# Two of four probability tiles turned by VectorE and transfers instead of TensorE, in 21 plain steps of a fused attention and expert kernel, with a new order of the plain steps

## The reference, cut to what matters

```python
q = (hidden_states @ Wq).reshape(B, Sq, H, D)          # H = 16 heads of D = 128
k = (encoder_hidden_states @ Wk).reshape(B, Skv, H, D)
v = (encoder_hidden_states @ Wv).reshape(B, Skv, H, D)
q = rmsnorm(q, gq)
k = rmsnorm(k, gk)
scores = jnp.einsum('bqhd,bkhd->bhqk', q, k) * scale
attn = jax.nn.softmax(scores, axis=-1)
out = jnp.einsum('bhqk,bkhd->bqhd', attn, v)
return out.reshape(B, Sq, H * D) @ Wo
```

## Time and profile before

| | |
|---|---|
| median of 3 runs | 1463.31 us |
| span of the profiled execution, first to last instruction | 1461.5 us |
| TensorE busy (matmul) | 1437.8 us, 98% |
| VectorE, ScalarE, GpSimd busy | 76%, 67%, 59% |
| granted TensorE clock, mean | 0.998 |

### The profile page before, as it was taken

The page is one execution under the profiler, slowest core; times in us unless marked ns, Lnnn a source line. Parts: engine busy times, 40 slices in busy tenths (PEclk is TensorE's granted clock), DMA queues, the critical chain, the costliest instruction groups (busy, mean ns, idle before and its releaser), DMA issues.

```text
span 1461.5 us, 23763 instructions
## 1 busy us (share of the span) xinstructions
PE 1437.8 (98%) x8086; PEld 1223.0 (84%) x8086; DVE 1107.0 (76%) x2100; ACT 977.5 (67%) x2224; POOL 864.5 (59%) x701
## 2 busy tenths in 40 slices
PE   8999999999999999999999999999999999999998
PEld 6778788888888888888888888888888888888887
DVE  7888777777777777777777777777777776787777
ACT  7864477777776667667676767667676765666664
POOL 4785555555554566666575757575666655664341
PEclk9999999999999999999999999999999999999999
DMA  8420011111111333434333433433434331321002
GB/s 325 159 66 16 22 44 45 57 44 44 44 44 44 139 124 126 149 108 147 124 129 127 139 123 127 139 117 132 136 115 144 125 126 36 107 82 37 8 1 87
DMA packets 55495, 142.74 MB, mean 98 GB/s; under 512 B 5392, under 2 KB 5392, under 8 KB 55376
## 3 DMA queue, kind: packets, MB, share of 16 engines
q1 hardware_dynamic: 51616, 128.90, 26.1%
q0 software_dynamic: 3760, 12.32, 3.0%
HBM read 126.79 MB, written 14.42 MB: 97 GB/s over the span
## 4 chain that ended last, share of the span: by engine, by line
PE 82%; DVE 7%; ACT 4%; POOL 4%; issue 2%; DMA 0%; ACTq 0%; SPq 0%; DVEq 0%; POOLq 0%
PE w_bank L505 10%; PE w_bank L507 10%; PE w_bank L506 10%; PE j_bank L505 9%; PE j_bank L507 9%; PE j_bank L506 9%; PE t_bank L573 7%; PE s_bank L505 4%; PE s_bank L507 4%; PE s_bank L506 4%; PE t_bank L538 2%; POOL q_scale L1855 2%; POOL wo_lo L1815 2%; ACT prob L927 1%; PE t_bank L657 1%
## 5 line engine op out<-in xcount | busy, mean ns | idle before, releaser
L927 ACT ACTIVATE prob<-s_bank,neg_bias,q_scale 128x512 f32<-128x512 f32 x255 | 198.0, 777 | 186.5 <-DVE neg_bias L1422 186.4
L1262 DVE TENSOR_TENSOR probT_lo<-t_bank,probT_hi 128x512 fp32r<-128x512 f32 x260 | 176.4, 689 | 168.4 <-ACT probT_hi L892 168.4
L1476 DVE SCALAR_TENSOR_TENSOR x_sb<-w_bank,inv_sum,x_sb 128x512 f32<-128x512 f32 x254 | 188.4, 744 | 0.0
L1401 DVE TENSOR_REDUCE neg_max<-s_bank 128x1 f32<-128x512 f32 x255 | 168.6, 682 | 0.9 <-PE s_bank L507 0.9
L1815 POOL TENSOR_TENSOR xnT_lo<-xnT_raw,xnT_hi 128x512 fp32r<-128x512 f32 (+2 forms) x47 | 126.5, 2693 | 61.5 <-ACT xnT_hi L892 61.5
L573 PE MATMUL t_bank<-ident,prob 128*128 128x128 f32 x1008 | 151.4, 273 | 1.3 <-ACT prob L927 1.1
L892 ACT CAST probT_hi<-t_bank 128x512 fp32r<-128x512 f32 x260 | 150.1, 590 | 1.8 <-PE t_bank L515 1.8
L1855 POOL TENSOR_TENSOR q_scale<-q_ss,minus_half 128x4 f32<-128x4 f32 x64 | 65.9, 1030 | 143.6 <-DVE q_ss L1414 143.6
L505 PE MATMUL j_bank<-wkv_lo,cT_hi 128*128 128x256 f32 x512 | 145.1, 283 | 0.7 <-DVE oT_lo L1262 0.4
L507 PE MATMUL j_bank<-wkv_hi,cT_lo 128*128 128x256 f32 x512 | 144.6, 282 | 0.0
L506 PE MATMUL j_bank<-wkv_hi,cT_hi 128*128 128x256 f32 x512 | 144.4, 282 | 0.0
(11 more groups left out here) (308 smaller groups left out, 4454.2 us busy)
## 6 DMA issues: line engine op xcount, KB each, us to landing
stage<-w SPq DMA_DIRECT2D x96, 256.0 KB, 3.4
xnT_raw<-w_gu SPq DMA_DIRECT2D x31, 704.0 KB, 4.8
cT_raw<-w_gu SPq DMA_DIRECT2D x31, 704.0 KB, 4.7
xnT_raw<-w_dn SPq DMA_DIRECT2D x16, 768.0 KB, 4.4
cT_raw<-w_dn SPq DMA_DIRECT2D x15, 768.0 KB, 4.7
planes<-bits SPq DMA_DIRECT2D x16, 512.0 KB, 4.8
y<-stage SPq DMA_DIRECT2D x31, 256.0 KB, 4.0
x_sb<-x SPq DMA_DIRECT2D x5, 1024.0 KB, 10.9
```

The costliest lines, as they stand in the source:

```text
L927: nc.scalar.activation(prob[:, i, :], score_bank(t, i)[:], ACT.Exp, bias=neg_bias[:, u % 2, i:i + 1], scale=q_scale[:, u % 2, i:i + 1], ac ...
L1262: return nc.vector.tensor_tensor(dst, src, hi, ALU.subtract)
L1401: nc.vector.tensor_reduce(neg_max[:, u % 2, i:i + 1], score_bank(t, i)[:], AX_X, ALU.max, negate=True).then_inc(own_max, 1)
L1476: nc.vector.scalar_tensor_tensor(out=here, in0=w_bank[0][:] if packed else out_bank(t, i)[:], scalar=inv_sum[:, w % 2, i:i + 1], in1=here, ...
```

## The change: two tiles by another way, a new order of the plain steps, and weights split a step ahead

1. In steps 3 to 18 and 58 to 62 (21 steps, `moved(u)` with u = t-1) tiles 0 and 1 of the probabilities are not turned by TensorE. Their exponentials are written with keys and groups in another order; VectorE turns 32 by 32 blocks in place (`turn_quads`, one instruction of 128 x 1024); SP stores the two tiles to a DRAM scratch (`store_pair`, 512 KB) and loads them back in four transfers of 32 partitions each, in rows of 512 B (`load_pair`); in the next step ScalarE copies them (`moved_hi`, 128 x 1024) and GpSimd subtracts (`moved_lo`, 128 x 1024).
2. `probT` now holds, in all steps, each tile as runs of 32 query columns; `values` reads 16 runs of 32 columns at a distance of 512 B as its moving operand.
3. All plain steps stand in a new order on TensorE, ScalarE, VectorE and SP. `values` writes `t_bank[1]` in them, where it wrote `j_bank[0]`.
4. The key and value weights of item t+1 are split in step t, where they were split at the head of step t+1, in the plain and in the packed steps.

```diff
+def moved(u):
+    return 3 <= u + 1 < T0 - 1 or T0 + NB + 7 <= u + 1 < NI - 1
+def turned_tiles(u):
+    return (2, 3) if moved(u) else range(NT)
...
+        probT_keys = [t[:, :, :].rearrange("p i s -> p (i s)").rearrange("p (q j c) -> p j q c", j=NT, c=QUAD)
+                      for t in probT]
...
+            def store_pair(u):
+                if not moved(u):
+                    return
+                sp.wait_ge(p_quads, MOVES[u] + 1)
+                wait(sp, p_moved, 16 * NT * MOVES[u])
+                sp.dma_start(turn_dram.rearrange("i p m -> p i m"), prob_pair).then_inc(p_stored, 16)
+            def load_pair(u):
+                if not moved(u):
+                    return
+                sp.wait_ge(p_stored, 16 * (MOVES[u] + 1))
+                for c in range(NT):
+                    sp.dma_start(prob[c * QUAD:(c + 1) * QUAD, 0:2, :].rearrange("a i (r m) -> a (i r) m", r=NT),
+                                 turn_dram.rearrange("i (r a) (c m) -> c a (i r) m", r=NT, c=NT)[c]).then_inc(p_moved, 16)
...
+                store_pair(t - 1)
+                load_pair(t - 1)
...
                 def values():
-                    need(pe, p_lo, 4, w, 4)
+                    wait(pe, p_lo, TILES[w + 1])
+                    wait(pe, pair_lo, MOVES[w + 1])
...
-                        last = product(j_bank[0][:], [a[:, w % 2, 1, j * P:(j + 1) * P] for a in kv],
-                                       [a[:, j, :] for a in probT], j == 0, j == NT - 1)
+                        last = product(whole_values(t)[:].rearrange("p (q c) -> p q c", c=QUAD),
+                                       [a[:, w % 2, 1, j * P:(j + 1) * P] for a in kv],
+                                       [a[:, j] for a in probT_keys], j == 0, j == NT - 1)
...
+                def moved_hi(v):
+                    if not moved(v):
+                        return
+                    act.wait_ge(p_moved, 16 * NT * (MOVES[v] + 1))
+                    need(act, pv_mm, 1, v - 1, 1)
+                    copy_hi(probT_pair(0), prob_pair).then_inc(pair_hi, 1)
...
+                def turn_quads():
+                    if not moved(u):
+                        return
+                    need(dve, p_exp, 4, u, 2)
+                    flat_pair = prob_pair.rearrange("p i s -> p (i s)")
+                    nc.vector.transpose(flat_pair, flat_pair).then_inc(p_quads, 1)
...
+                def moved_lo(v):
+                    if not moved(v):
+                        return
+                    pool.wait_ge(pair_hi, MOVES[v] + 1)
+                    lower(probT_pair(1), prob_pair, f32(probT_pair(0))).then_inc(pair_lo, 1)
```

More of the change, by code:

```diff
@@ L782, in step @@
                 scores(1)
-                if not (up and down):
+                if not packed:
+                    project_down()
+                    key_value(0, (0,))
+                    query_squares()
+                    key_value(0, (1,))
+                    late_turn()
+                    key_value(1)
+                    values()
+                    if t == 2:
+                        table()
+                    scores(2)
+                    scores(3)
+                    query((0, 1))
+                    project_out(0)
+                    probs(0)
+                    project_out(1)
+                    probs(1)
+                    probs(2)
+                    query((2, 3))
+                    key_turn()
+                    project_out(2)
+                    probs(3)
+                    project_out(3)
+                    return
+                if not down:
                     query_squares()
@@ new lines, in step @@
+                if t == T0 - 1:
+                    dve.wait_ge(x0_out, 16)
+                    dve.wait_ge(rstd_ready, NMOMENTS // NT + 1)
+                    for i in range(NT):
+                        normalised(i)
+                turn_quads()
+                if t == 2:
+                    tokens()
+                values_lo()
+                take(0)
+                if t == T0 - 2:
+                    statistics(0, 1, NMOMENTS + 1)
+                maximum(2)
+                shift(2)
@@ new lines, in step @@
+                maximum(3)
+                shift(3)
+                add(0)
+                add(1)
+                values_rows()
+                if t == T0 - 2:
+                    statistics(0, 2, NMOMENTS + 2)
+                    statistics(0, 3, NMOMENTS + 3)
+                    for i in range(NT):
+                        mean_variance(0, i, NMOMENTS + i)
+                if t == T0 - 1:
+                    nc.vector.memset(h_row[:, I:], 0.0).then_inc(pad_ready, 1)
+                take(1)
@@ L1715, in _ @@
+                probs_lo(0)
+                probs_lo(1)
+                probs_lo(2)
+                query_lo()
+                key_lo()
+                if t == NI - 1:
+                    last_squares_lo()
+                take(2)
+                add(2)
+                take(3)
+                probs_lo(3)
+                if not deferred(t):
+                    add(3)
             for kind, b in DVE_ORDER:
@@ L1934, in step @@
                 values_lo()
+                if t + 1 < NI and fresh(t + 1):
+                    lower_wkv(t + 1)
                 if t == T0 - 1:
```

290 lines of the change are left out of this document (139 added, 151 removed).

## The result

The changed kernel takes 1471.24 us, the median of 13 runs (1467.96 to 1478.23), where the kernel before took 1464.8 in 13 runs on the same chip: a ratio of 1.0054, 95% interval 1.004 to 1.0068. The forecast was 1436 us, in a range of 1427 to 1450. The change makes the kernel slower by 6 us, and the prediction was wrong in size and in sign.

A forecast was written before the change was run, and what follows sets the result against it. TensorE was taken to bound the kernel. Gains of 21.0 (steps 3 to 18), 4.2 (58 to 62) and 2.1 (52 to 57) made 27.3: 1461.5 - 27.3 = 1434.2, plus 1.8 for the median, 1436 us; range 1427 to 1450.

The forecast's parts named there:

- The step that failed: Plain steps that move no tile: steps 52 to 57 gain 2.1 us, steps 2, 19, 51 and 63 left unchanged.
- 0.25 left over: Delay on TensorE in a late plain step: of 0.6 us, 0.25 was kept as remaining under the new order.
- What it removes on TensorE: Two turned tiles less at 0.44 us each: 0.88 us in each of 21 steps, 18.5 us in all.
- the period of moved steps: Length of a step that moves tiles: 16.3 us for a late one, 16.0 for the others.
- The round trip: Pair's loop through DRAM and back, step to step: 15.6 to 16.6 us against a 16.35 us TensorE step; just in time.
- the long case: Pair's loop when the store waits behind the weights' bytes: 1 us more, 16.6 us.
- the first rival: Moved steps: the pair's loop through DRAM sets the period, fresh steps take 17.2 us, kernel 1455; chance 0.18.
- The four loads: Loads of 128 KB issued some 0.4 us apart, the last landing like a small one: 4.0 us.
- The rival's own terms: Loads landing one behind the other: 10.8 us in place of 4.0, loop 22.4 in 21 steps, about 1560; chance 0.02.
- The values' operand: Runs of 32 columns read by 756 `values` matmuls: taken to cost 0, at most 0.12 us each, 91 us.
- the slower rival: Runs of 32 slow the 756 `values` matmuls: up to 1527 us, deciding from 0.036 us a matmul; chance 0.07.
- Weights a step ahead: Packed steps, earlier split of key and value weights: costed at nothing, up to 0.5 us in each of 10 steps otherwise.

The follow-up runs named there:

- Experiments 1: Changed kernel with steps 19, 51 to 57 and 63 back in the order of the kernel before, `values` in its old bank there: 1459.2 us, ratio 0.9973.
- 4: Changed kernel with no tile going by transfers: new order in all plain steps, four tiles turned on TensorE in each; 1520.8 us, measured once.
- experiment 6: Changed kernel with tile 2 turned behind the second half of the queries in plain steps that turn four tiles on TensorE: 1461.8 us, measured once.
- the fastest kernel: Changed kernel with old order in steps 51 to 57, runs of 32 only for moved items, pair ahead of weights, tile 2 later in 2, 19, 63: 1443.16 us.
- experiment 7: Changed kernel with the store and loads of the pair issued on SP ahead of the query and output weights: 1466.97 us, ratio 1.0015.
- 2: Changed kernel with the runs of 32 columns only in the 21 moved items, other items in one run of 512: 1469.16 us, ratio 1.0035.

## Why the prediction was wrong, step by step

- **The step that failed:** "Steps 52 to 57 [...] the work is 17.0 - 0.44 = 16.55, with 0.25 left over 16.8: 2.1. The remaining plain steps (2, 19, 51, 63) I leave." It put the new order in those steps down as a small gain or nothing. Measured: +16.8 for steps 50 to 57 where -2.1 was forecast, and +1.9, +0.8 and +1.7 for step 19, step 63 and steps 1 and 2 where 0 was: 23.3 of the 35.2 us between the forecast sum and the profiled result. (The others are the start, 3.2, steps 3 to 18, 5.5, and the packed steps, 3.1, with 0.1 in the rest.) I placed the new list for a moved step only, two tiles in it, and carried its "0.25 left over" to steps with four. It could have been seen ahead: the order of the changed kernel shows two adds and a copy of the value rows ahead of tile 0's subtraction on VectorE, and tile 2 on the same bank. Experiments 1, 4 and 6 show it: with the old order back the loss is gone, with no tile moved it stands in every step, and with tile 2 alone shifted more than half of the wait goes and a third of the loss. So the order is shown as the cause of nearly the whole (14.8 of 16.8 us), and the wait of tile 2 by itself as the cause of that third; for the rest it is the longest wait on the list, 13.5 of 16.7 us.
- **What it removes on TensorE, and the period of moved steps:** right. With the store ahead of the weights late steps take 16.27 (16.3), steps 16 and 17 15.82 (16.0), the first and the last of the sixteen 16.7 and 16.9, and all sixteen 260.5, against 259.6 in the sum.
- **The round trip:** its parts were right and its verdict half right. "Just in time, with nothing to spare in the long case" was the finding, and then the long case was costed at nothing. The store behind the weights took 4.0 in the median (forecast 4.5, quiet 3.5; measured quiet 2.8), and the steps where it came late cost 4.5 us in steps 3 to 18. So the first rival came true in a few steps, beside the forecast.
- **The four loads:** last landing 1.81 - 0.45 + 2.7 = 4.1 after the first issue, forecast 4.0. The rule of the Trainium skill, page "DMA: Bandwidth & Descriptors", section "Rules for kernel authors", that ranges of partitions share the engines, may hold for their bytes; as a rule on time the trace doesn't bear it out, since four loads issued within 1.8 us each took 2.7, and the 9 us estimated from the page did not come. The page's 2 us for the fixed part are a fit to transfers that GpSimd issues, and these are SP's. (The rival's own terms, a step of 22.4 in 21 steps, come to 1567, not to "about 1560".)
- **The values' operand:** taken at 0, measured at 0.009 to 0.011 us a matmul, about 4 us in all. The mechanism of the slower rival exists, at a quarter of its deciding point of 0.036. The Trainium skill, page "SBUF — State Buffer", section "Specifications (TRN2)", has it cost nothing by the rule of two hits a 16-byte line; the measurement differs by 4% of a matmul's pace, and decides.
- **Weights a step ahead:** no cost seen. With the runs of 32 taken away the packed steps take 23.50, against 23.48 before; the first packed step is 0.6 shorter.
- **The rival for slower** named the wrong mechanism: a slower operand, not an order that two kinds of step share. Of the chance of 0.09 for slower, 0.07 rested on it and 0.02 on loads that land one behind the other; none rested on the order.

What stays open: in the fastest kernel steps 1 and 2 are 1.0 us longer than before and steps 50 to 57 1.7, of which the mark is 0.7 each; the rest wasn't followed up. Nor were the 9 us by which the stretch of experiment 6 stays behind the old order. How often the clock falls behind a wait, and in which runs, is open too.

## What to carry to other kernels

When one list of instructions serves two kinds of step, walk the new order through each kind, above all the one the change isn't made for: ask of every shared buffer who reads it last and what stands ahead of that reader in its engine's list. A sum that says "just in time" is a term and not a zero; first put the urgent transfer ahead of those that have a whole step. Busy time falling while the span grows says at once that it is a wait; the list of waits of one stretch names it in a line.

## What the runs showed of the hardware

- **A wait can be followed by a fall of the clock.** In the run of experiment 7, the wait of tile 2 in step 55 was followed by matmuls at the lower level, 1.2 GHz, and so was the one in step 56 (TensorE, both waits):

```profile
1299.34 0.63 PE L639 MATMUL t_bank<-ident,prob 128*128 128x128 f32 x4 [2.09 <-DVE probT_lo L1370]
...
1320.73 0.98 PE L639 MATMUL t_bank<-ident,prob 128*128 128x128 f32 x4 [2.45 <-DVE probT_lo L1370]
```

The stretches behind the first (the third figure from the end is the granted clock, 1.00 being 2.4 GHz):

```profile
1299.80:1301.50 1.70, 1.70 (x8) 1.33 (x7) 0.69 (x1) 0.59 (x1) 0.00 (x0) 0.67 0.00 0
1301.50:1303.20 1.70, 1.70 (x8) 1.41 (x7) 0.47 (x1) 0.82 (x2) 0.00 (x0) 0.50 0.00 0
1304.90:1306.60 1.70, 1.70 (x10) 1.41 (x9) 1.70 (x3) 0.23 (x1) 1.55 (x2) 1.00 0.03 10
```

The two steps took 1.5 and 1.1 us more than the same ones of the changed kernel, whose clock stayed at 1.00 behind the same waits of 2.09 and 2.45. So it happens in some runs only. The profiles of experiments 1, 2 and 4 show six more falls, behind waits of 1.79 to 2.88 us. In the 13 runs of the changed kernel a mean clock of 0.999 goes with spans of 1466.2 to 1468.0 us, and 0.992 or 0.993 with 1474.4 to 1476.4; the kernel before stays at 0.996 to 0.999 in its latest 15 runs. Which idle spell is followed by a fall wasn't settled.

- **A block transposition on VectorE is cheap:** 32 by 32 blocks of 128x1024 float32 in place take 1.25 us, 1.2 ns an element of a partition, less than two subtractions of 512 (2 x 0.69).
- **A transfer pays for those issued just ahead of it:** the 512 KB store took 2.8 us in the median when issued first, and 4.0 behind two weight transfers of 256 KB issued within 1 us ahead of it. In the changed kernel the loads went out 3.9 to 5.6 us behind a store with weights ahead of it, and 2.8 to 3.4 behind one without.
